# Layer 2's expert router as eight wide products into four partition groups, with its small tables fetched one phase sooner

## What is computed

```python
x = x + _L0_ffn_ref(_L0_cond_ref(x, cond_1024, ...), ...)
x = x + _L1_ffn_ref(_L1_cond_ref(x, cond_1024, ...), L1_ffn_Wr, L1_ffn_br, L1_ffn_W1, L1_ffn_b1, L1_ffn_W2, L1_ffn_b2)
x = x + _L2_ffn_ref(_L2_cond_ref(x, cond_1024, ...), ...)
x = x + _L3_ffn_ref(_L3_cond_ref(x, cond_1024[:, None, :], ...), ...)

def _L1_ffn_ref(x, Wr, br, W1, b1, W2, b2):      # D = 256, E = 8 experts, F = 1024
    xt = x.reshape(B * S, D)
    logits = (xt @ Wr + br) / TEMP               # [2048, 8]: the router
    gates = entmax_bisect(logits)                # 25 bisection steps over the 8 experts
    gates = jnp.where(gates > THRESH, gates, 0.0)
    h = jax.nn.relu(jnp.einsum('td,edf->etf', xt, W1) + b1[:, None, :])
    y = jnp.einsum('etf,efd->etd', h, W2) + b2[:, None, :]
    out = jnp.einsum('etd,te->td', y, gates)     # every expert sees every token
```

## Time and profile before

| what | value |
|---|---|
| median of 3 runs | 2480.6 us |
| the profiled execution's own time | 2481.35 us |
| its span in the profile | 2479.6 us |
| mean granted clock of TensorE | 0.896 of full speed |
| TensorE (PE) busy | 2102.7 us, 85% |
| VectorE (DVE) busy | 1353.4 us, 55% |
| ScalarE (ACT) busy | 985.4 us, 40% |
| GpSimd (POOL) busy | 245.2 us, 10% |
| layer 2's expert phase | from 668.8 to about 1396 us |

### The profile page before, as it was taken

The page is one execution under the profiler, slowest core; times in us unless marked ns, Lnnn a source line. Parts: engine busy times, 40 slices in busy tenths (PEclk is TensorE's granted clock), DMA queues, the critical chain, the costliest instruction groups (busy, mean ns, idle before and its releaser), DMA issues. The chain is left out here.

```text
span 2479.6 us, 34352 instructions
## 1 busy us (share of the span) xinstructions
PE 2102.7 (85%) x13371; PEld 1687.4 (68%) x13371; DVE 1353.4 (55%) x2579; ACT 985.4 (40%) x1954; POOL 245.2 (10%) x207
## 2 busy tenths in 40 slices
PE   6788789999799999999999884779956867785886
PEld 5477668888687888888888774469944654554554
DVE  2589555778575444443443214456637456454885
ACT  2143255555353444444444220234523345464222
POOL 1144200000000000000000002028820000000000
PEclk7789889999899999999999995589977866998989
DMA  2375221233113121111100000255355001000000
GB/s 78 94 236 158 65 69 55 83 102 102 36 34 74 46 35 34 37 49 35 34 1 1 10 3 1 67 185 141 83 110 136 2 9 44 18 18 35 1 9 26
DMA packets 111587, 146.01 MB, mean 59 GB/s; under 512 B 6756, under 2 KB 94755, under 8 KB 111172
## 3 DMA queue, kind: packets, MB, share of 16 engines
q1 hardware_dynamic: 101316, 129.99, 17.4%
q0 software_dynamic: 10112, 13.85, 3.2%
HBM read 121.83 MB, written 21.99 MB: 58 GB/s over the span
## 5 line engine op out<-in xcount | busy, mean ns | idle before, releaser
L1601 DVE TENSOR_TENSOR m_h_lo<-m_hf,m_h_hi 128x512 fp32r<-128x512 f32 x256 | 172.1, 690 | 358.8 <-ACT m_hf L1576 356.9
L1573 ACT ACTIVATE m_h_hi<-m_h_ps,m_bT 128x512 fp32r<-128x512 f32 x256 | 177.0, 691 | 367.3 <-PE m_h_ps L396 347.7
L1576 ACT ACTIVATE m_hf<-m_h_ps,m_bT 128x512 f32<-128x512 f32 x256 | 175.0, 684 | 0.0
L600 POOL DMA_INDIRECT token_sums<-e_y,slot_row x56 | 145.7, 2602 | 159.5 <-DVE e_y L703 147.3
L665 ACT ACTIVATE e_h_hi<-e_h_ps,e_b1T 128x320 fp32r<-128x320 f32 (+1 forms) x128 | 78.0, 609 | 168.6 <-PE e_h_ps L396 163.5
L1313 DVE TENSOR_TENSOR c_h_lo<-c_hf,c_h_hi 128x512 fp32r<-128x512 f32 x120 | 82.2, 687 | 74.2 <-ACT c_hf L1272 73.1
L719 DVE TENSOR_TENSOR e_h_lo<-e_hf,e_h_hi 128x320 fp32r<-128x320 f32 (+1 forms) x128 | 74.0, 589 | 77.8 <-ACT e_hf L668 76.3
L1840 POOL MEMSET n_bias<- 128x256 f32 x1 | 0.3, 312 | 1082.4 <-POOLq L59 1082.4
L1269 ACT ACTIVATE c_h_hi<-c_h_ps,c_b 128x512 fp32r<-128x512 f32 x88 | 62.2, 707 | 109.3 <-PE c_h_ps L396 108.8
L396 PE MATMUL m_y_ps<-m_h_hi,l_w_1hi 128*128 128x512 f32 x256 | 100.4, 392 | 3.5 <-issue 3.5
L396 PE MATMUL m_y_ps<-m_h_hi,l_w_0hi 128*128 128x512 f32 x256 | 99.7, 389 | 1.4 <-ACT m_gT L1587 1.4
(11 more groups left out here) (644 smaller groups left out, 5603.7 us busy)
## 6 DMA issues: line engine op xcount, KB each, us to landing
cT<-in_L_ffn_W_dram SPq DMA_DIRECT2D x30, 1024.0 KB, 5.3
res<-in_L_cond_ew_dram SPq DMA_DIRECT2D x22, 1024.0 KB, 5.3
cT<-in_L_ffn_w_dram SPq DMA_DIRECT2D x16, 1024.0 KB, 6.2
res<-gates_rows SPq DMA_DIRECT2D x8, 1024.0 KB, 14.8
l_mod<-modulation_rows SPq DMA_DIRECT2D x16, 512.0 KB, 6.6
token_rows<-d_tok SPq DMA_DIRECT2D x2, 2112.0 KB, 9.6
token_sums<-res SPq DMA_DIRECT2D x2, 2048.0 KB, 7.5
res<-token_sums SPq DMA_DIRECT2D x8, 512.0 KB, 5.6
```

The costliest lines, as they stand in the source:

```text
L600: pool.indirect_dma_start(out=sums, out_offset=bass.IndirectOffsetOnAxis(ap=st.slot_row[0:r, e, j:j + 1], axis=0), in_=y[0:r, e % 2, j, :] ...
L1573: act.activation(hs[0][:, f, :], h_ps[:, f % HB, :], ACT.Relu, bias=bT[:, at:at + 1])
L1576: act.activation(hf[:, f % HB, :], h_ps[:, f % HB, :], ACT.Relu, bias=bT[:, at:at + 1]).then_inc(act_done, 1)
L1601: dve.tensor_tensor(hs[1][:, f, :], hf[:, f % HB, :], hs[0][:, f, :].bitcast(F32), ALU.subtract).then_inc(h_ready, 1)
```

## The change

The router's roles are swapped. `wr`, filled with zeros to 32 columns, is the stationary operand, and a block of 512 tokens the moving one; block g's product goes to partitions 32g to 32g + 31 of one PSUM bank. That makes 4 blocks by 2 slabs, 8 matmuls of 512 columns. The logits come out turned (8 rows per block), so ScalarE copies them (`logitsT`), four 128x128 transposes on TensorE turn them back, and VectorE adds the bias in four instructions, one per group, in place of one. The transposes stand behind the first slab of `up(0)`; VectorE's `bounds` waits for them.

The bias transposes now stand ahead of the router, and the four small tables (`wr`, `bias`, and the two tables of expert biases) are loaded by SyncE at the end of the conditioning phase's stream, behind expert 0's weights. GpSimd clears `wr` at the start of that phase. The tables' tiles are allocated outside both phases.

```diff
--- before.py
+++ after.py
@@ -1073,7 +1073,7 @@
...
 def l1_cond_phase(nc, sem, st, srcT, accT, w1s, w2s, gate_w, gate_b, time_w, time_b, ew1, eb1, ew2, eb2, sw1, sb1, sw2, sb2,
-                  next_w1, next_w2):
+                  next_w1, next_w2, next_small):
@@ -1142,6 +1142,8 @@
...
             sp.dma_start(w2_raw, next_w2.rearrange("(c p) d -> p c d", p=P)).then_inc(w2_in, 16)
+            sp.wait_ge(b_turned, 1)
+            next_small.load(sp, st)
@@ -1160,6 +1162,7 @@
...
             pool.memset(seen[:, 2, 0:HEAD_END], 0.0).then_inc(const1, 1)
+            pool.memset(next_small.wr[:, :, :], 0.0).then_inc(next_small.wr_zero, 1)
@@ -1428,7 +1431,29 @@
...
-def l1_ffn_phase(nc, sem, st, srcT, accT, w1s, w2s, Wr, br, W1, b1, W2, b2):
+GC = P // NB
+
+
+class L1FfnSmall:
+
+
+    def __init__(self, nc, sem, mem, Wr, br, b1, b2):
+        sb = lambda name, shape: mem.enter_context(nc.sbuf_tensor("m1_" + name, shape, F32))
+        self.from_memory = (Wr, br, b1, b2)
+        self.wr, self.bias, self.b2rows = sb("wr", [P, KC, GC]), sb("bias", [P, E8]), sb("b2rows", [E8 * KC, P])
+        self.wr_zero, self.wr_in, self.bias_in, self.b_in, self.b2_in = (
+            sem("m1_" + x) for x in "wr_zero wr_in bias_in b_in b2_in".split())
+
+    def load(self, sp, st):
+        Wr, br, b1, b2 = self.from_memory
+        sp.wait_ge(self.wr_zero, 1)
+        sp.dma_start(self.wr[:, :, 0:E8], Wr.rearrange("(c p) e -> p c e", p=P)).then_inc(self.wr_in, 16)
+        sp.dma_start(self.bias[:, :], br.partition_broadcast(P)).then_inc(self.bias_in, 16)
+        sp.dma_start(st.b1rows[:, :], b1.rearrange("e (c p) -> (e c) p", p=P)).then_inc(self.b_in, 16)
+        sp.dma_start(self.b2rows[:, :], b2.rearrange("e (c p) -> (e c) p", p=P)).then_inc(self.b2_in, 16)
+
+
+def l1_ffn_phase(nc, sem, st, srcT, accT, w1s, w2s, small, W1, W2):
@@ -1442,11 +1467,13 @@
...
         bT = sb("bT", [P, E8 * FC])
-        b2rows, b2T = sb("b2rows", [E8 * KC, P]), sb("b2T", [P, E8 * KC])
+        b2T = sb("b2T", [P, E8 * KC])
+        logitsT = sb("logitsT", [P, BLK])
         w1_raw = srcT[:, 0, :].rearrange("p (c f) -> p c f", c=KC)
...
         mix = st.res[:, :, :].rearrange("p t d -> p (t d)").rearrange("p (i n) -> p i n", i=2)
-        wr, bias = sb("wr", [P, KC, E8]), sb("bias", [P, E8])
+        wr, bias, b2rows = small.wr, small.bias, small.b2rows
+        wr_in, bias_in, b_in, b2_in = small.wr_in, small.bias_in, small.b_in, small.b2_in
         logits, diff, gates = sb("logits", [P, NT, E8]), sb("diff", [P, NT, E8]), sb("gates", [P, NT, E8])
@@ -1456,11 +1483,11 @@
-        l_ps = y_ps[:, 1, 1, 0:NT * E8]
+        lT_ps, l_ps = y_ps[:, 1, 0, :], y_ps[:, 1, 1, :]
...
@@ -1469,11 +1496,6 @@
...
-            sp.dma_start(wr[:, :, :], Wr.rearrange("(c p) e -> p c e", p=P)).then_inc(r_in, 16)
-            sp.dma_start(bias[:, :], br.partition_broadcast(P)).then_inc(r_in, 16)
-            sp.dma_start(st.b1rows[:, :], b1.rearrange("e (c p) -> (e c) p", p=P)).then_inc(b_in, 16)
-            sp.dma_start(b2rows[:, :], b2.rearrange("e (c p) -> (e c) p", p=P)).then_inc(b2_in, 16)
-
@@ -1516,6 +1538,14 @@
...
                     last.then_inc(up_done, 1)
+                    if n == 0:
+                        turn_logits()
+
+            def turn_logits():
+                pe.wait_ge(products_kept, 1)
+                for j in range(TPB):
+                    last = pe.transpose(l_ps[:, j * P:(j + 1) * P], logitsT[:, j * P:(j + 1) * P], st.ident[:, :])
+                last.then_inc(logits_made, 1)
@@ -1533,21 +1563,21 @@
...
-            pe.wait_ge(r_in, 32)
-            for t in range(NT):
-                for k in range(KC):
-                    last = pe.matmul(l_ps[:, t * E8:(t + 1) * E8], srcT[:, k, t * P:(t + 1) * P], wr[:, k, :], start=(k == 0),
-                                     stop=(k == KC - 1))
-            last.then_inc(logits_made, 1)
             pe.wait_ge(b_in, 16)
...
             pe.transpose(h_ps[:, HB - 1, E8 * FC:E8 * (FC + KC)], b2rows[:, :], st.ident[0:E8 * KC, 0:E8 * KC]).then_inc(b_turned, 1)
+            pe.wait_ge(wr_in, 16)
+            for k in range(KC):
+                for g in range(NB):
+                    last = pe.matmul(lT_ps[g * GC:(g + 1) * GC, :], wr[:, k, :], srcT[:, k, blk(g)], start=(k == 0),
+                                     stop=(k == KC - 1), skip_group_check=True)
+            last.then_inc(products_made, 1)
             pe.wait_ge(b_kept, 2)
...
                 if u == 1:
-                    pe.wait_ge(logits_kept, 1)
+                    pe.wait_ge(logits_kept, NB)
                 if u == NB - 1:
@@ -1564,6 +1594,8 @@
...
             act.activation(b2T[:, :], h_ps[:, HB - 1, E8 * FC:E8 * (FC + KC)], ACT.Copy).then_inc(b_kept, 1)
+            act.wait_ge(products_made, 1)
+            act.activation(logitsT[:, :], lT_ps, ACT.Copy).then_inc(products_kept, 1)
             act.wait_ge(b_kept, 2)
@@ -1646,10 +1678,12 @@
...
                 dve.wait_ge(logits_made, 1)
-                dve.wait_ge(r_in, 32)
-                dve.tensor_tensor(logits[:, :, :], l_ps.rearrange("p (t e) -> p t e", e=E8), bc(bias[:, :], 1, NT),
-                                  ALU.add).then_inc(logits_kept, 1)
-                dve.wait_ge(logits_kept, 1)
+                dve.wait_ge(bias_in, 16)
+                made = l_ps.rearrange("p (j g e) -> p g j e", j=TPB, g=NB)
+                for g in range(NB):
+                    dve.tensor_tensor(logits[:, g * TPB:(g + 1) * TPB, :], made[:, g, :, 0:E8], bc(bias[:, :], 1, TPB),
+                                      ALU.add).then_inc(logits_kept, 1)
+                dve.wait_ge(logits_kept, NB)
                 link(dve.tensor_scalar(logits[:, :, :], logits[:, :, :], 0.5, None, ALU.mult))
@@ -3075,10 +3109,11 @@
...
         w2s = [[sb(f"w2_{i}{x}", [P, FC, D]) for x in ("hi", "lo")] for i in range(2)]
+        small = L1FfnSmall(nc, sem, mem, *w("L1_ffn_", "Wr", "br", "b1", "b2"))
         l1_cond_phase(nc, sem, st, st.cT, st.cT2, w1s, w2s,
                       *w("L1_cond_", "gate_w", "gate_b", "time_w", "time_b", "ew1", "eb1", "ew2", "eb2", "sw1", "sb1", "sw2", "sb2"),
-                      a["L1_ffn_W1"][0], a["L1_ffn_W2"][0])
-        l1_ffn_phase(nc, sem, st, st.cT2, st.cT, w1s, w2s, *w("L1_ffn_", "Wr", "br", "W1", "b1", "W2", "b2"))
+                      a["L1_ffn_W1"][0], a["L1_ffn_W2"][0], small)
+        l1_ffn_phase(nc, sem, st, st.cT2, st.cT, w1s, w2s, small, *w("L1_ffn_", "W1", "W2"))
...
 def adaln_ffn_4_layers(nc, a, out):
```

More of the change, by code:

```diff
@@ L1458, in l1_ffn_phase @@
         y_ps = mem.enter_context(nc.psum_tensor("m1_y_ps", [P, 2, KC, BLK], F32))
-        l_ps = y_ps[:, 1, 1, 0:NT * E8]
+        lT_ps, l_ps = y_ps[:, 1, 0, :], y_ps[:, 1, 1, :]
         t_ps = y_ps[:, 1, 0, 0:P]
-        names = ("r_in b_in b2_in b_turned b_kept logits_made logits_kept w1_in w2_in w1_hi w2_hi w1_split w2_split x_hi x_ready "
+        names = ("b_turned b_kept products_made products_kept logits_made logits_kept w1_in w2_in w1_hi w2_hi w1_split w2_split x_hi x_ready "
                  "up_done act_done h_ready y_done y_free y_kept gates_set gates_turned gates_kept gates_out mix_used chain").split()
-        (r_in, b_in, b2_in, b_turned, b_kept, logits_made, logits_kept, w1_in, w2_in, w1_hi, w2_hi, w1_split, w2_split, x_hi, x_ready,
+        (b_turned, b_kept, products_made, products_kept, logits_made, logits_kept, w1_in, w2_in, w1_hi, w2_hi, w1_split, w2_split, x_hi, x_ready,
          up_done, act_done, h_ready, y_done, y_free, y_kept, gates_set, gates_turned, gates_kept, gates_out, mix_used, chain) = (
```

## The result

The changed kernel is slower, by 0.5%. Its median is 2496.3 us (5 runs, 2495.84 to 2497.05) against 2482.2 us for the kernel before in the same session (5 runs, 2478.63 to 2487.5): ratio 1.0048, 95% interval 1.0035 to 1.006. The forecast was 2467.3 us. The profiled execution spans 2495.2 us, 15.6 more than the 2479.6 of before.

The account below looks back on a forecast made before the run. The bound was one serial path at the phase border (tables, router, transposes, copies), then matmuls. `up(1)` would start 13.8 us sooner, or 12.2 with a low clock; 13.3 was taken: 2480.6 - 13.3 = 2467.3 us, range 2463.5 to 2472.

Parts of the forecast that it names:

- The tables: At the phase border, tables loaded a phase sooner land in time, so TensorE's wait of 3.09 us goes.
- Rival (e): At the border the tables would still be awaited, costing 3.1 us: 2470.4 us; 2 in 100.
- The router: Ahead of `up(0)`, 16 records run four side by side: 3.41 us plus 0.1 in place of 13.75.
- (a): In the router only neighbouring records overlap: 7.7 us in place of 3.4, say 2470.5 us; 6 in 100.
- (b): In the router no records overlap: 13.65 us, gain 3.6, 2477.0 us; 4 in 100.
- the slow one (d): Router records run in series, each awaiting its predecessor and its weights: 24.9 us, 2489.8 us; 2 in 100.
- The clock: In `up(0)`, the clock rises as it begins, gaining up to 1.77 us, or only behind slab 0.
- VectorE gives back: After the router, later `bounds` puts first `h_low` 12.7 us sooner, not 13.6; TensorE waits 1.1 us before `up(1)`.
- Rival (c): At TensorE's later 3.5 us wait, the wait doubles and the clock drops: 3.5 + 1.8 us, 2472.6 us; 5 in 100.
- Behind it each distance is as before: After `up(1)` starts, the rest of the expert phase keeps its spacing, so the 13.3 us gain is kept.
- what is saved moves the end of the phase: From `up(0)` on matmuls set the time, so time saved ahead moves the phase's end by as much.
- The range: For the whole kernel, 2463.5 us (full gain 13.8, lowest run) to 2472 us, just short of Rival (c).

Follow-up runs that it names:

- the one with 1024 bytes: Changed kernel plus 224 unused bytes per partition behind the four tables' tiles, 1024 bytes together: 2468.83 us, and 2468.5 us when run again.
- the kernel before with 32 bytes: Kernel before plus one unused tile of 32 bytes per partition between layer 2's weights and its x and h tiles: 2511.4 us.

## Why the prediction was wrong

By its own steps:

- **The tables**, 3.1 us hidden: right. With the wide router, early tables bring `up(0)` 3.3 us closer to the border (7.5 and 4.2); with the narrow one, 2.9 (17.8 and 14.9). Rival (e) falls, since no table is awaited at the border.
- **The router**, 3.41 + 0.1 us for 16 records at the low clock, four side by side: measured 3.52. `up(0)` forecast 4.2 us behind the border (673.1 by the old scale), measured 4.17. The 0.029 us per record of layer 3's narrow form carried over to 512 columns. The rivals (a), 7.7 us, and (b), 13.65, and the slow one (d) fall. The sum's 0.853 us for a record is (3.62 - 1.06) / 3 by the earlier trace rows, at clock 0.50, and the rounds after are 0.85 apart at the same clock.
- **The clock** rose at 678.3, 3.4 us after the first router record (674.87) and just ahead of `up(0)` (678.39), as in the more hopeful of the two cases.
- **VectorE gives back**: first `h_low` forecast 9.5 us behind the border (678.4), measured 9.45; `up(1)` forecast 27.5 (696.4), measured 27.4. Of the 1.1 us that TensorE was to wait for `m_x_lo` 0.16 is left in the changed kernel, because its slower matmuls come later themselves, and 0.7 in the one with 1024 bytes. Rival (c) falls in its main part, with 3.5 us at the place where there were 3.5 before; the low clock behind that wait did last longer, 6.8 us in place of 3.4, which cost 0.8 us where that rival had 1.8.
- **"Behind it each distance is as before"** is the step that failed, and with it the sentence that "what is saved moves the end of the phase". `up(1)` to the last `cT` went from 684.6 to 705.3 us, and the conditioning phase, for which the sum has no term at all, from 349.8 to 355.7. What stood in its place is a slower matmul: 0.2331 us from start to start where it was 0.2264, because the new tables moved x and h to 32 bytes off the weights: with 224 bytes more behind them it was 0.2262 again, with the tables ahead of the weights 0.2264. Of what would make it wrong, the text had named the right sign, a growing distance from `up(1)` to the end, but gave it no price and no cause. The working treated the change as a change of instructions. It is also one of allocation: three tiles made ahead of phases that allocate behind them move the x and h tiles of layer 2 by 800 bytes in the program as built, and the 0.227 us per matmul that the working used for slab 0 was taken as a constant of the form. The addresses could be had from the program without a run; that they bear on the time no row of before could show, since the tiles that its L396 matmuls read all lie at 0 modulo 256. What could have been had is a rival that says so: "layer 2's x and h tiles move by 800 bytes", with a price per matmul times some 4500 matmuls.
- **The range**: its lower end, 2463.5, doesn't come out of its own terms. 2478.63 - 13.8 - 1.77 is 2463.1, and the 1.77 of the clock is in the 13.8 already, which has slab 0 and `up(0)` at full clock.

In size: the forecast gain was 13.3 us, the kernel with the tables first gained 14.5 (ratio 0.993 to 0.9957), and its 2469.07 us lie within the forecast range. The changed kernel lost 26.6 us by the profile beside that gain, so the terms of the sum were right and what it left out decided. The version that beats both kernels is the changed one with its tables' tiles ahead of the weights; the one with 224 bytes of padding does as well (2468.5 and 2468.83).

## What to carry to other kernels

A new tile is a change to every tile that is allocated behind it: before and after, compare the start addresses of what the matmuls read, the weights and the streamed tile of each pair, and keep their distance as it was or at a multiple of 256 bytes, which cost nothing in these runs (0.2262 to 0.2264 us per matmul). When a whole phase is slower though nothing in it changed and TensorE is busy without a gap in both profiles, count its records in a window of equal length before looking at waits. A test with one pad costs one line, and a test on the kernel before tells the address from all the rest of the change.

## What the runs showed of the hardware

- A 512-column float32r matmul with 128 x 128 weights started every 0.2262 to 0.2264 us where streamed tile and weights lie a multiple of 256 bytes apart, and every 0.2287 to 0.2331 us where they lie 32, 64, 96 or 128 bytes off one, at the same granted clock of 1.00. Both moved by 32 bytes cost nothing (0.2264 us, 2480.87 us in all). Whether float32 matmuls or fewer columns pay as well, none of these runs tried.
- Where the distance is 64, a third of the cost is paid, not half: 1312 records in 300 us between 1325 and 1287.
- At one and the same pause of 3.5 us in a dense stream, the granted clock was 0.50 for 3.4 us in the profile before, for 6.8 in the one after, and not at all in that of the kernel before with 32 bytes, where the 8 us behind the pause have a clock of 1.00. Over the 48 matmuls behind it that is 1.7, 2.5 and 0.1 us, so by this estimate spans of single profiles differ by up to 2.4 us here from the clock alone.
- Sixteen float32 records of 512 columns in four groups of partitions ran in four rounds of 0.85 us at clock 0.50, 3.52 us in all, so side by side, and 4 x 0.853 = 3.41 us leaves 0.1 us for all else.
